# Layer 1's odd 96 rows first: gate and 32 of up's rows in one weight, up's other 64 in full fp32, both token halves side by side on the array's columns

## What is computed

```
approx_up = hidden_states @ up_w.T
gate_pre = hidden_states @ gate_w.T
delta = gate_pre - local_point
...
ffn_out = jax.nn.silu(hidden_states @ ffn_gate_w.T) * (hidden_states @ ffn_up_w.T) @ ffn_down_w.T
return approx_out + ffn_out
```

## Time and profile before

| | |
|---|---|
| time, median of 3 runs | 411.65 us (411.63 to 411.87) |
| the profiled execution | 412.71 us, of which the span is 410.8 us |
| TensorE busy | 401.8 us, 98% |
| VectorE, GpSimd, ScalarE busy | 325.1, 290.1, 267.4 us (79%, 71%, 65%) |

### The profile page before, as it was taken

The page is one execution under the profiler, slowest core; times in us unless marked ns, Lnnn a source line. Parts: engine busy times, 40 slices in busy tenths (PEclk is TensorE's granted clock), DMA queues, the critical chain, the costliest instruction groups (busy, mean ns, idle before and its releaser), DMA issues.

```text
span 410.8 us, 5355 instructions
## 1 busy us (share of the span) xinstructions
PE 401.8 (98%) x1770; PEld 327.9 (80%) x1770; DVE 325.1 (79%) x383; ACT 267.4 (65%) x372; POOL 290.1 (71%) x228
## 2 busy tenths in 40 slices
PE   7999999999999999999999999999999999999993
PEld 5888888888877888888888888888888877888872
DVE  3629989779888986999998799987779989935035
ACT  5575666677676847466956658888769777732613
POOL 0077998877978489936993366799999998954430
PEclk9999999999999999999999999999999999999998
DMA  7994101100204362103043000000000000000202
GB/s 258 409 408 146 53 14 51 28 26 0 53 3 123 89 224 69 27 0 104 1 131 146 0 2 1 2 0 0 2 2 0 2 0 0 2 0 2 102 0 102
DMA packets 10042, 26.48 MB, mean 64 GB/s; under 512 B 1248, under 2 KB 1632, under 8 KB 9760
## 3 DMA queue, kind: packets, MB, share of 16 engines
q1 hardware_dynamic: 9584, 25.37, 18.2%
q10 hardware_dynamic: 432, 0.79, 0.7%
HBM read 24.06 MB, written 2.10 MB: 64 GB/s over the span
## 4 chain that ended last, share of the span: by engine, by line
PE 95%; DMA 2%; DVE 1%; ACT 0%; issue 0%; POOLq 0%; SPq 0%; DVEq 0%; ACTq 0%
PE PS L1257 32%; PE PS L1258 31%; PE PS L1259 31%; DMA h<-xT 2%; PE PS L1361 1%; POOLq L249 0%; SPq L522 0%; ACT R L567 0%; DVE stats L933 0%; DVE R L928 0%; DVE x_lo L1041 0%; ACT x_hi L567 0%; ACT std L784 0%; DVE mv L959 0%; DVE std L972 0%
## 5 line engine op out<-in xcount | busy, mean ns | idle before, releaser
L1182 POOL TENSOR_SCALAR level<-side 128x1024 f32<-128x1024 int8 (+2 forms) x119 | 129.7, 1090 | 27.1 <-ACT side L567 13.0
L855 DVE TENSOR_TENSOR PS<-PS,level 128x1024 f32<-128x1024 f32 (+2 forms) x102 | 120.1, 1178 | 23.1 <-POOL level L1182 19.1
L1257 PE MATMUL PS<-x_hi,w_hi 128*128 128x512 f32 (+1 forms) x348 | 135.8, 390 | 0.9 <-DVE x_lo L1041 0.9
L1259 PE MATMUL PS<-x_hi,w_lo 128*128 128x512 f32 (+1 forms) x348 | 135.6, 390 | 0.0
L1258 PE MATMUL PS<-x_lo,w_hi 128*128 128x512 f32 (+1 forms) x348 | 135.5, 389 | 0.0
L567 ACT ACTIVATE side<-Q 128x1024 int8<-128x1024 f32 (+2 forms) x84 | 80.1, 997 | 17.2 <-DVE PS L851 15.2
L1257 PEld LDWEIGHTS PS<-x_hi,w_hi 128*128 128x128 f32 (+1 forms) x348 | 64.5, 185 | 16.1 <-issue 1.7
L1212 POOL TENSOR_TENSOR l_lo<-h,l_hi 128x512 fp32r<-128x512 f32 (+1 forms) x42 | 57.6, 1379 | 27.3 <-ACT l_hi L567 26.4
L1259 PEld LDWEIGHTS PS<-x_hi,w_lo 128*128 128x128 f32 (+1 forms) x348 | 64.5, 185 | 14.5
L1258 PEld LDWEIGHTS PS<-x_lo,w_hi 128*128 128x128 f32 (+1 forms) x348 | 64.5, 185 | 14.4
L1257 PE MATMUL PS<-x_hi,l_hi 128*128 128x512 f32 x144 | 56.1, 390 | 0.0
(11 more groups left out here) (100 smaller groups left out, 510.6 us busy)
## 6 DMA issues: line engine op xcount, KB each, us to landing
Q<-w SPq DMA_DIRECT2D x10, 512.0 KB, 13.8
raw<-w_in SPq DMA_DIRECT2D x9, 512.0 KB, 12.3
raw<-w_out SPq DMA_DIRECT2D x14, 256.0 KB, 2.6
raw<-w SPq DMA_DIRECT2D x5, 512.0 KB, 3.8
R<-xN SPq DMA_DIRECT2D x2, 1024.0 KB, 5.4
raw<-w_fuse SPq DMA_DIRECT2D x7, 256.0 KB, 2.6
out<-R SPq DMA_DIRECT2D x7, 256.0 KB, 2.0
h<-xT SPq DMA_DIRECT2D x2, 512.0 KB, 8.1
```

Of the source, the lines that this page charges most:

```text
L855: v.tensor_tensor(total, total, level_of(s), ALU.add).then_inc(s_add, 1)
L1182: g.tensor_scalar(level_of(s), side_of(s), LIMITS[k][1], LIMITS[k][0], ALU.min, ALU.max).then_inc(s_level, 1)
L1257: t_.matmul(dst, a_hi, b_hi, start=start, stop=False)
L1259: return t_.matmul(dst, a_lo, b_hi, start=False, stop=stop)
```

## The change

The odd group of 96 rows is now f = 0 in layer 1, on the gate's and up's side and on the down projection's, and the full groups follow. For f = 0 the host packs the gate's 96 rows and up's rows 64 to 95 as one weight of 128 columns, which is split as before (512 elements a partition in place of 1024), and up's rows 0 to 63 behind it, which aren't split. `project_first` makes 12 matmuls a half with the first; `project_up` makes 8 fp32 matmuls of 64 columns of weight with the raw weight and the raw x, for half 0 into partitions 0 to 63 and for half 1 into 64 to 127 of bank 5. All 8 stand in pair 0, between its gate and pair 1. VectorE multiplies h in two parts for pairs 0 and 1, pair 3 waits for the h of both, and SP's load into the first group's slot waits for pair 0 too. (Hunks of the diff without all of their context.)

```diff
@@ -39,6 +39,10 @@
+REST, LEFT = F1 % P, 64
+assert 2 * REST - P == LEFT
@@ -240,9 +244,18 @@
+def rows1(f):
+    return REST if f == 0 else P
+def first_row1(f):
+    return REST + (f - 1) * P if f else 0
     kind, f = job
-    return P if kind == "fuse" else rows(f, F1) if kind == "out" else rows(f, F2)
+    return P if kind == "fuse" else rows1(f) if kind == "out" else rows(f, F2)
@@ -317,11 +330,15 @@
             if kind == "in":
-                return P, 2 * DC * rows(f, F1)
+                return P, 2 * DC * rows1(f)
+        def split_shape(j):
+            return (P, DC * P) if JOBS[j] == ("in", 0) else job_shape(j)
         def raw_parts(j):
-            p, n = job_shape(j)
+            p, n = split_shape(j)
@@ -436,9 +453,18 @@
+        UP_BANK = 5
+        def parted_up(i):
+            _, half, bank = pair_of(1, i)
+            return [(slice(LEFT, REST), PS[REST:P, bank, :]),
+                    (slice(0, LEFT), PS[half * LEFT:(half + 1) * LEFT, UP_BANK, :])]
             f, half, _ = pair_of(layer, i)
-            p = rows(f, F1 if layer == 1 else F2)
+            p = rows1(f) if layer == 1 else rows(f, F2)
@@ -498,13 +524,17 @@
                     wait_split(sp, j - RAW_SLOTS)
+                    if j - RAW_SLOTS == JOB["in", 0]:
+                        wait_pairs_done(sp, 1, 1)
                 if kind == "in":
-                    src = w_in[:, f * 1024:f * 1024 + n]
+                    first = 2 * DC * first_row1(f)
+                    src = w_in[:, first:first + n]
                 else:
-                    src = w_out[f[1] * P:f[1] * P + p, :]
+                    src = w_out[first_row1(f[1]):first_row1(f[1]) + p, :]
@@ -882,7 +912,12 @@
                 dve.wait_ge(s_silu, i + 1 + (2 * C1 if layer == 2 else 0))
-                v.tensor_tensor(dst, PS[0:dst.shape[0], pair_of(layer, i)[2] + 1, :], dst, ALU.mult).then_inc(s_h, 1)
+                if layer == 1 and i < 2:
+                    for to, up_rows in parted_up(i):
+                        last = v.tensor_tensor(dst[to, :], up_rows, dst[to, :], ALU.mult)
+                    last.then_inc(s_h, 1)
+                else:
+                    v.tensor_tensor(dst, PS[0:dst.shape[0], pair_of(layer, i)[2] + 1, :], dst, ALU.mult).then_inc(s_h, 1)
@@ -1044,7 +1079,7 @@
             wait_raw_slot(dve, 1)
-            v.tensor_tensor(lo1, w_raw(1), hi1.bitcast(F32), ALU.subtract).then_inc(s_wlo0, 1)
+            v.tensor_tensor(lo1, w_raw(1)[:, 0:DC * P], hi1.bitcast(F32), ALU.subtract).then_inc(s_wlo0, 1)
@@ -1278,9 +1313,27 @@
+            def project_first(half, bank):
+                wh, wl = (in_slot(w, JOB["in", 0], DC * P).rearrange("p (c m) -> p c m", c=DC) for w in (w_hi, w_lo))
+                for c in range(DC):
+                    xs = slice(half * HALF, (half + 1) * HALF)
+                    last = product(PS[:, bank, :], wh[:, c, :], wl[:, c, :], x_hi[:, c, xs], x_lo[:, c, xs], c == 0,
+                                   c == DC - 1)
+                return last
+            def project_up():
+                w = w_raw(JOB["in", 0])[:, DC * P:2 * DC * REST].rearrange("p (c m) -> p c m", c=DC)
+                for c in range(DC):
+                    for half in range(2):
+                        last = t_.matmul(PS[half * LEFT:(half + 1) * LEFT, UP_BANK, :], w[:, c, :],
+                                         xT_raw[:, c, half * HALF:(half + 1) * HALF], start=c == 0, stop=c == DC - 1)
+                return last
                 f, half, bank = pair_of(layer, i)
-                m = rows(f, F1 if layer == 1 else F2)
+                m = rows1(f) if layer == 1 else rows(f, F2)
@@ -1291,7 +1344,7 @@
-                        pe.wait_ge(s_h, i - 2)
+                        pe.wait_ge(s_h, max(2, i - 2))
@@ -1302,6 +1355,12 @@
                     pe.wait_ge(s_xl, X_PARTS + (TILES if half == 0 and i < 2 else TT))
+                if layer == 1 and i < 2:
+                    last = project_first(half, bank)
+                    if half == 0:
+                        last = project_up()
+                    last.then_inc(s_pair, 1)
+                    return
@@ -1433,11 +1492,14 @@
         parts = []
-        for f in range(-(-width // P)):
-            m = min(P, width - f * P)
+        if width == F1:
+            gate, up = (w[:REST].reshape(REST, DC, P) for w in ws)
+            parts += [x.transpose(2, 1, 0).reshape(P, -1) for x in (np.concatenate([gate, up[LEFT:]]), up[:LEFT])]
+            ws = [w[REST:] for w in ws]
+        for f in range(width // P):
+            m = P
         return np.ascontiguousarray(np.concatenate(parts, axis=1))

```

## The result

| | before | changed |
|---|---|---|
| median | 411.75 us (411.36 to 412.45, 8 runs) | 410.75 us (410.27 to 410.84, 8 runs) |
| ratio | | 0.9973 (0.9964 to 0.9983) |
| the profiled execution | 412.71, span 410.8 | 410.27, span 408.2 |

The change is worth 1.1 us (0.27% of 411.75, by the interval 0.17 to 0.36%). The forecast of 411.0 lies 0.25 from the 410.75 measured; but the 0.6 us that it gave the change is about half of what the change brings, and the overlap is the one of rival 1.

What follows compares the result with a forecast made beforehand. TensorE, 98% busy, was taken as the bound: 5.44 us removed, less block, borders and pair 3's wait, left 0.75, and after pair 8 about 0.6. From 412.71 that gave 412.1, or 411.05 as median, stated 411.0; range 410.1 to 412.3.

Steps and rivals of the forecast that it cites:

- rival 1: Full gain: the fp32 halves overlap wholly or the chain to pair 3 is shorter; 409.75 to 410.5 us, chance 0.30.
- removed slots: Odd group's gate and up in layer 1: 24 of 48 TensorE products go, 0.2267 us each, 5.44 us removed.
- the block: The 8 added fp32 matmuls between pair 0's gate and pair 1: 9 steps of 0.444 us, 4.00 us.
- TensorE's own sum: TensorE alone: 5.44 removed less 4.00 and 0.08 on entry, 1.36 us gained, less some 0.1 on leaving.
- wait ahead of pair 3, with the slow slot behind it: TensorE at pair 3 waits for pair 1's h, with the second slot 0.08 longer: costs 0.5 us.
- left at pair 3: Gain remaining when pair 3 effectively starts, at 33.54 instead of 34.29: 0.75 us.
- pair 8: TensorE there waits for GpSimd's later w_lo of the fifth group: 0.1 us and 0.08 behind it.
- Rival 3: Gain lost later: GpSimd, held up by VectorE, brings pair 8's w_lo about 1 us later; 412.0 us, chance 0.12.
- the chain is rigid: ScalarE, GpSimd and VectorE work from L605 to pair 1's h shifts as a whole, by 0.96 us.
- SP's load for the sixth group: Load now waits for pair 0, near 24.9 us; first used at 72.4 us, so priced at nothing.
- the moved order, with the last group's longer splits: Odd group first adds no slots; last splits take 0.5 us more on GpSimd near 108 us, in gaps: nothing.
- 4.75 - B: Gain at pair 3 for a block of B us, through the chain to pair 1's h; above 4.75 us the change loses.

Runs made afterwards that it cites:

- half_by_half: Changed kernel with the 8 fp32 matmuls ordered as all of half 0, then all of half 1: 412.32 us, ratio 1.0012 to the kernel before.
- own_banks: Changed kernel with half 1's up rows in bank 1 instead of bank 5, so pair 3 waits for pair 0's h alone: 410.67 us, ratio 0.9969.
- one_part: Changed kernel without the first of VectorE's two h multiplications for pairs 0 and 1: one profile, 391.17 us from pair 0's first product to the end.
- order_only: Kernel before with only the odd group moved first, its 48 split gate and up products kept: 412.01 us, ratio 0.9998.
- own_banks_level: own_banks with a GpSimd level, and the normalisation ahead of it, moved behind the w_lo that pair 8 reads: 414.25 us, ratio 1.0061.
- own_banks_swap: own_banks with the w_lo that pair 8 reads put ahead of an l_lo on GpSimd: 410.63 us, ratio 0.9971.
- swap_only: Changed kernel with the same GpSimd exchange as own_banks_swap: one profile, 391.18 us from pair 0's first product to the end.
- two_by_two: Changed kernel with the fp32 matmuls ordered two chunks of half 0, two of half 1, and again: one profile, 391.27 us from pair 0's first product.

## Why the prediction was right, and where it was off

| step | predicted | profile after |
|---|---|---|
| removed slots | 5.44 | 5.44 (12 of pair 0's gate end at 19.41 + 0.23) |
| entry to the block | 0.08 | 0.09 |
| the block | 4.00 (9 steps of 0.444) | 3.58 (8 steps) |
| leaving it | 0.1 | 0.11 (23.31 to 23.65 in place of 0.227) |
| TensorE's own sum | 1.36 - 0.1 | 1.66 |
| wait ahead of pair 3, with the slow slot behind it | 0.5 | 0.45 + 0.11 |
| left at pair 3 | 0.75 | 1.10 |
| pair 8 | 0.1 + 0.08 | 0 |
| all | 0.6 | 1.0 to 1.1 |

**The step that was off** is the overlap: "I take 9 slots, 4.00 us: if starts stay in order, a record waits only for the record before it on its own columns". Starts don't stay in order. In the changed kernel a pair of records starts 6 to 7 ns apart in every one of 8 steps, though each matmul's second record should stand ahead of the other half's first; half_by_half shows it however a matmul is cut. That is one step less, 0.43 us. A record took 0.429 us and not 0.444, 0.12 over 8 steps, but the first step (0.48) and the last (0.53) are 0.05 and 0.10 longer, which eats that. Rival 1 had this overlap, and its formula with the measured block gives 4.75 - 3.58 = 1.17 against the 1.10 measured. I had given it 0.30 against the forecast's 0.42: the rows of before could not tell them apart, and I chose wrongly.

**What was luck.** The stated range, 410.1 to 412.3 us, held the forecast and rivals 1 and 3 alike, so a time inside it says nothing for the 9 steps. The gain in the traces, 1.0 to 1.1 us, lies outside the 0.3 to 0.8 that the forecast named, and the time above rival 1's 409.75 to 410.5. The 411.0 came as near as 0.25 us since it was counted from 411.65, the median of three runs, where eight gave 411.75, and 411.05 was rounded down. Of the signs named for the profile after, the 16 records and the wait of pair 3 came; the 9 steps of 4.0 us and the wait of pair 8 did not.

**What held.** The wait of pair 3 was found in the right place, of the right size and for the right reason: own_banks and one_part each take it away by another link of its cause. That the chain is rigid held too. The profile after starts pair 0 1.06 us earlier (16.917 and 17.974); in the time of before, L635 starts at 24.98, where I had 25.47, and GpSimd's three levels at 27.16, where I had 27.65: 0.49 earlier each, the block's 0.42 and 0.07 more. The h of pair 1 lasts 1.40 and not 1.28, and starts 1.26 behind L885's start in place of 1.14, so 0.26 of the 0.49 is left at its end (33.05, predicted 33.31). VectorE's next instruction ends 1.08 us behind GpSimd's w_lo in both kernels (34.59 and 33.51; 33.98 and 32.90), which fits the prediction's reading that it is held by it.

**Pair 8** did not wait since the chain behind the block was earlier by the same half us: GpSimd's w_lo ends at 59.13, TensorE starts at 59.39. Its 0.18 was the block's error seen a second time. That it was the next wait in line was right: own_banks and one_part run into exactly that w_lo. After it stands VectorE's l_lo at 138 us, which I had priced at 0 since I had "found GpSimd, ScalarE and VectorE each waiting for TensorE's results in every stage"; for what was gained in the changed kernel that holds, for 0.5 us more it doesn't.

**At nothing.** SP's load for the sixth group and the moved order, with the last group's longer splits, cost nothing: no wait for a weight of layer 1 is in the waits of TensorE, and order_only is at 0.9998. Rival 3 did not come; its kind of trouble was met in own_banks_level.

No version that was run beats the changed kernel by more than can be measured. own_banks, one_part, own_banks_swap, swap_only and two_by_two lie between 391.17 and 391.31 in the rest, and TensorE's own sum would allow 392.41 - 1.66 = 390.75. What paces VectorE up to 138 us, and whether it can be brought forward without own_banks_level's losses, stays open.

## What to carry to other kernels

Before pricing an added block on the critical engine, price its side effects as a chain with the block's length as a variable (here 4.75 - B): it gives the break-even at once, and the error of a wrong B can be read off. When a wait is relieved, look for the next instruction that is just in time, and measure slack from an anchor inside the same execution, since the start scatters by more than the effect. Small matmuls that leave half of the columns idle can be paired on disjoint columns, but they must alternate closely in program order: all of one tile first gave back half of what the overlap saves (5.35 us against 3.58 and 7.01).

## What the runs showed of the hardware

- Two fp32 matmuls of 64 columns on disjoint columns start 6 to 7 ns apart and each keeps its 0.429 us a record (512 columns, granted clock 1.0): 3.58 us against 7.01 on the same columns. The TensorEngine Tiling (Array Packing) page of the Trainium skill (Theoretical Speedup) gives up to a factor of 2 for this size; the two blocks here give 1.96, and the drain that the page states at a change of tiling mode (Key Properties) fits the 0.09 and 0.11 us on entering and leaving, which no run here takes apart.
- The TensorE: Matmul & The Clock Gate page of the Trainium skill (Part 3: Packing small matmuls, The mechanism) says that matmuls keep the program's order in start and end, with no reordering. half_by_half doesn't agree: a record passed three waiting ones (its start at 21952 is ahead of theirs, from 22376 ns on).
- One instruction of VectorE over 96 partitions, made as two over 32 and 64, takes 1.40 us; one of 64 partitions takes 0.69 (one_part), and one of 128 takes 0.68, 512 fp32 elements a partition each.
- One dequantisation level and the normalisation ahead of it, put behind one w_lo in GpSimd's order, cost 3.6 us (own_banks_level against own_banks).
